# A fused retention and mixture-of-experts layer: routing at the end of VectorE's rounds, expert biases loaded ahead of rows, and one normalisation ahead of the last expert slot's activations

## The reference, cut to what matters

```python
xn = layernorm(x)
q, k, v = xn @ W_q.T, xn @ W_k.T, xn @ W_v.T              # 16 heads of 16
attn = einsum('bihd,bjhd->bhij', q, k) * decay / sqrt(16) # decay: gamma_h ** (i - j), causal
y = einsum('bhij,bjhd->bihd', attn, v)
yn = (y - y.mean((1, 3))) / sqrt(y.var((1, 3)) + eps)     # over time and head width
a = (yn * gn_weight + gn_bias) @ W_o.T
probs = softmax(xn @ gate_w.T + gate_b); top 2 of 8
f = sum over the two experts of prob * (relu(xn @ w1[e] + b1[e]) @ w2[e] + b2[e])
out = x + a + f
```

## Time and profile before

| what | us |
|---|---|
| median of 3 runs | 731.72 (730.7 to 731.83) |
| the profiled execution's own time | 733.6 |
| its span | 731.2 |
| PE busy | 694.6 (95%) |
| DVE busy | 579.1 (79%) |
| ACT busy | 486.0 (66%) |
| mean granted TensorE clock | 0.994 of full speed |

### The profile page before, as it was taken

One profiled execution on the slowest core, in us unless ns is written; L12 is line 12 of the kernel. 1 busy time (PEld: TensorE's weight loads), 2 busy tenths in 40 slices (PEclk: granted clock), 3 DMA queues, 4 the chain that ended last, 5 costly groups with the idle time before them and its releaser, 6 DMA issues.

```text
span 731.2 us, 19479 instructions
## 1 busy us (share of the span) xinstructions
PE 694.6 (95%) x6564; PEld 652.8 (89%) x6564; DVE 579.1 (79%) x1090; ACT 486.0 (66%) x883; POOL 287.4 (39%) x229
## 2 busy tenths in 40 slices
PE   3899999999999999999999999999999999999976
PEld 2677777887888999999999999999999999999975
DVE  6778889887887896887787878787878787888655
ACT  3645433443445887878787787878787878788690
POOL 3300006688650143543535353535344444434200
PEclk9999999999999999999999999999999999999999
DMA  9960113533750978787878788878887888878249
GB/s 303 373 234 31 58 52 116 167 117 124 238 180 7 372 187 252 204 268 193 264 195 262 199 256 223 232 230 230 233 230 234 223 245 214 261 186 264 34 144 324
DMA packets 67632, 149.17 MB, mean 204 GB/s; under 512 B 12560, under 2 KB 46096, under 8 KB 57488
## 3 DMA queue, kind: packets, MB, share of 16 engines
q1 hardware_dynamic: 53872, 130.53, 52.4%
q0 software_dynamic: 13728, 18.23, 15.2%
HBM read 111.22 MB, written 36.46 MB: 202 GB/s over the span
## 4 chain that ended last, share of the span: by engine, by line
PE 67%; DMA 11%; issue 9%; DVE 6%; POOL 3%; ACT 3%; SPq 1%; DVEq 0%; POOLq 0%; ACTq 0%
PE ps L816 26%; PE ps L731 25%; DMA xs_rows<-xn_rows,rows 6%; PE ps L778 3%; DMA sum_rows<-arena_f,pair_slot 2%; PE ps L993 2%; PE ps L800 2%; PE ps L864 2%; PE ps L843 2%; PE ps L854 1%; POOL sum_rows L490 1%; DMA xn_rows<-x 1%; PE ps L787 1%; PE ps L824 1%; POOL xs_rows L470 1%
## 5 line engine op out<-in xcount | busy, mean ns | idle before, releaser
L816 PE MATMUL ps<-arena_r 128*128 128x256 f32 (+1 forms) x1872 | 229.7, 282 | 0.3 <-DVE arena_r L1234 0.3
L731 PE MATMUL ps<-arena_r 128*128 128x256 f32 x1776 | 224.2, 286 | 3.0 <-DVE arena_r L1331 3.0
L816 PEld LDWEIGHTS ps<-arena_r 128*128 128x128 f32 x1872 | 225.9, 192 | 0.7 <-issue 0.7
L731 PEld LDWEIGHTS ps<-arena_r 128*128 128x128 f32 x1776 | 216.9, 193 | 4.0 <-DVE arena_r L1331 2.4
L488 POOL TENSOR_TENSOR fence_out<-eps_col 128x1 f32<-128x1 f32 x39 | 77.9, 1998 | 273.7 <-DVE arena_f L1301 273.7
L542 ACT ACTIVATE arena_r<-arena_f 128x2048 fp32r<-128x2048 f32 x77 | 143.7, 1920 | 0.2 <-DMA arena_f<-w 0.2
L490 POOL DMA_INDIRECT sum_rows<-arena_f,pair_slot x74 | 118.9, 1606 | 16.6 <-issue 15.5
L655 ACT ACTIVATE arena_f<-ps,arena_f 128x256 f32<-128x256 f32 (+1 forms) x156 | 63.8, 461 | 88.7 <-PE ps L816 69.5
L1322 DVE TENSOR_TENSOR arena_r<-arena_f,arena_r 128x2048 fp32r<-128x2048 f32 x39 | 89.3, 2291 | 32.2 <-ACT arena_r L542 32.1
L1216 DVE TENSOR_TENSOR arena_f<-ps,cst 128x512 f32<-128x512 f32 x128 | 84.6, 683 | 6.3 <-PE ps L843 5.8
L1331 DVE TENSOR_TENSOR arena_r<-arena_f,arena_r 128x512 fp32r<-128x512 f32 (+1 forms) x78 | 53.3, 686 | 44.3 <-ACT arena_r L664 44.2
(11 more groups left out here) (156 smaller groups left out, 837.4 us busy)
## 6 DMA issues: line engine op xcount, KB each, us to landing
arena_f<-w SPq DMA_DIRECT2D x78, 1024.0 KB, 5.7
xs_rows<-spare_rows SPq DMA_DIRECT2D x35, 260.0 KB, 3.9
arena_f<-xs_rows SPq DMA_DIRECT2D x35, 260.0 KB, 3.1
arena_f<-b SPq DMA_DIRECT2D x39, 128.0 KB, 3.1
xn_rows<-x SPq DMA_DIRECT2D x8, 512.0 KB, 9.0
sum_rows<-x SPq DMA_DIRECT2D x8, 512.0 KB, 3.8
arena_f<-sum_rows SPq DMA_DIRECT2D x8, 512.0 KB, 7.5
out<-arena_f SPq DMA_DIRECT2D x16, 256.0 KB, 6.4
```

The costliest lines, as they stand in the source:

```text
L731: last = pe.matmul(out_ap, lhs(a), rhs(b), start=start and n == 0, stop=stop and n == 2, **kw)
L816: last = pe.matmul(ps[:, H_BANK[hp], o * rows:(o + 1) * rows], w1_r[par][:, a, at:at + P], xs_r[:, b, k * rows:(k + 1) * rows], start=(m = ...
```

## The change

It has three parts.

1. VectorE's routing pieces stand at the end of a round, behind the fourth masked score, where they stood behind `new_state`. They begin in round 0 rather than 1, so each piece but the last runs one round earlier; `gate_values` gets round 4 of its own, and both `rows_of_pairs` run in round 10. `counts_after` lies at another place of the same buffer, since its old place is overwritten by the output of tile 8.
2. SyncE issues the biases of slot sl+1 ahead of the rows of slot sl+2.
3. ScalarE normalises half batch 0 and makes its high part ahead of the `hidden` steps of the last slot (38), and VectorE runs `ys_gated` of that slot ahead of `low_half(1)`.

```diff
@@ -200,7 +200,7 @@
 
         w_raw = [ff(KC * cols) for cols in (2 * D, D, D)]
         x_grp_t = ff(2, KC, GRP * P)
-        counts_after = x_grp_t[:, 0, 0, 0:NT * E].rearrange("p (t e) -> p t e", t=NT)
+        counts_after = x_grp_t[:, 1, 1, NT * E:2 * NT * E].rearrange("p (t e) -> p t e", t=NT)
         ones_te = x_grp_t[:, 0, 1, 0:NT * E]
         logit_t = sb("logit_t", [P, 2, P])
         stats = sb("stats", [P, 2, GRP, 6])
@@ -417,9 +417,10 @@
             def slot_step(sl, par):
                 if within(sl + 2, NS):
                     weights_load(sl + 2, par)
-                    rows_load(sl + 2, par)
                 if within(sl + 1, NS):
                     bias_load(sl + 1, 1 - par)
+                if within(sl + 2, NS):
+                    rows_load(sl + 2, par)
 
             run_steps(sp, 0, NS, 2, NBIG - 3, slot_step)
 
@@ -663,10 +664,32 @@
                 rows = P * row_tiles(sl)
                 nc.scalar.activation(h_r[:, 0, hp * 2 * rows:(hp + 1) * 2 * rows], h_f[hp][:, 0:2 * rows], ACT.Copy).then_inc(s["h_h"], 1)
 
+            scale = gn_ab[:, 0].rearrange("p b h c -> p (b h) c")
+            shift = gn_ab[:, 1].rearrange("p b h c -> p (b h) c")
+
+            def norm_scale(hb):
+                for c in range(KC):
+                    nc.scalar.activation(y_t[:, hb * 4:hb * 4 + 4, c], y_t[:, hb * 4:hb * 4 + 4, c], ACT.Identity,
+                                         scale=scale[:, hb:hb + 1, c], bias=shift[:, hb:hb + 1, c]).then_inc(s["yn_f"], 1)
+
+            def norm_high(hb):
+                act.wait_ge(s["yn_f"], hb * 2 + 2)
+
+                wait(act, s["o_psum"], hb - 3)
+                nc.scalar.activation(yn_r[hb % 4][:, 0].rearrange("p c (t i) -> p t c i", t=4), y_t[:, hb * 4:hb * 4 + 4],
+                                     ACT.Copy).then_inc(s["yn_h"], 1)
+
             def slot_step(sl, par):
                 if within(sl + 1, NS):
                     w_high(0, sl + 1, 1 - par)
+                if isinstance(sl, int) and sl == NS - 1:
+                    act.wait_ge(s["gn_ab"], 2)
+                    act.wait_ge(s["y_home"], 16)
+                    norm_scale(0)
                 act.wait_ge(s[f"bias_in{par}"], (sl - par) * 16 + 32)
+                if isinstance(sl, int) and sl == NS - 1:
+                    act.wait_ge(s["ys_psum"], NS - 1)
+                    norm_high(0)
                 hidden(sl, par, 0)
                 for hp in range(1, FC // 2):
                     hidden(sl, par, hp)
@@ -698,27 +721,9 @@
                 slot_step(sl, sl % 2)
 
 
-            act.wait_ge(s["gn_ab"], 2)
-
-            act.wait_ge(s["ys_psum"], NS - 1)
-            scale = gn_ab[:, 0].rearrange("p b h c -> p (b h) c")
-            shift = gn_ab[:, 1].rearrange("p b h c -> p (b h) c")
-
-            act.wait_ge(s["y_home"], 16)
-
-            def norm_half(hb):
-
-                for c in range(KC):
-                    nc.scalar.activation(y_t[:, hb * 4:hb * 4 + 4, c], y_t[:, hb * 4:hb * 4 + 4, c], ACT.Identity,
-                                         scale=scale[:, hb:hb + 1, c], bias=shift[:, hb:hb + 1, c]).then_inc(s["yn_f"], 1)
-                act.wait_ge(s["yn_f"], hb * 2 + 2)
-
-                wait(act, s["o_psum"], hb - 3)
-                nc.scalar.activation(yn_r[hb % 4][:, 0].rearrange("p c (t i) -> p t c i", t=4), y_t[:, hb * 4:hb * 4 + 4],
-                                     ACT.Copy).then_inc(s["yn_h"], 1)
-
-            for hb in range(2 * B):
-                norm_half(hb)
+            for hb in range(1, 2 * B):
+                norm_scale(hb)
+                norm_high(hb)
 
 
         @block.tensor
@@ -1158,14 +1163,16 @@
                 V.tensor_copy(expert_of[:], slot_expert[:]).then_inc(s["route_done"], 1)
 
             def routing(i):
-                if i == 1:
+                if i == 0:
                     shifted_logits()
+                elif i == 1:
+                    first_expert()
                 elif i == 2:
-                    first_expert()
+                    next_peaks()
                 elif i == 3:
-                    next_peaks()
+                    second_expert()
                 elif i == 4:
-                    second_expert()
+                    gate_values()
                 elif i == 5:
                     tokens_upto()
                     tokens_of_experts()
@@ -1179,9 +1186,8 @@
                     rows_of_halves()
                 elif i == 10:
                     rows_of_pairs(0)
-                    gate_values()
+                    rows_of_pairs(1)
                 elif i == 11:
-                    rows_of_pairs(1)
                     experts_of_slots()
 
 
@@ -1248,8 +1254,6 @@
                     tokens_low(i + 1, 1 - par)
                 if within(i - 1, NT - 1):
                     new_state(i - 1)
-                if route:
-                    routing(i)
                 if stats > 1:
                     output_stats(i - LATE, early=True)
                 if isinstance(i, int) and i == NT - 1:
@@ -1268,6 +1272,8 @@
                     queries(i + 1, 1 - par)
                 if within(i, NT):
                     masked_scores(i, 3)
+                if route:
+                    routing(i)
 
 
             for g in range(-1, NG):
@@ -1413,8 +1419,8 @@
                     V.tensor_tensor(pair, pair, ps[:, hb % 3 * 2 + q, :], ALU.add).then_inc(s["out_sb"], 1)
 
             low_half(0)
+            ys_gated(NS - 1, (NS - 1) % 2)
             low_half(1)
-            ys_gated(NS - 1, (NS - 1) % 2)
             low_half(2)
             low_half(3)
             for hb in range(2 * B):
```

## The result

The changed kernel takes 794.62 us (median of 6 runs, 787.86 to 806.7), the kernel before beside it 731.74. The ratio is 1.0812, with a 95% interval of 1.0761 to 1.0863: **8% slower**. Forecast were 722.9 us.

A forecast was written before the change was run, and what follows sets the result against it. TensorE, busy 95% of the span, bounds the kernel, so time is gained where it idles or something else carries the end. 4.6 + 0 + 4.24 = 8.84 us off 731.72 gives 722.9 us; 8 in 10 range 720.5 to 726.0.

The forecast's parts named there:

- Part 1: Attention: routing pieces hide behind VectorE's existing waits, so GpSimd's scatters start at 106.4 instead of 111.02, 4.6 us gained.
- The two long pieces: Attention: the `rows_of_pairs` pair in round 10 and `experts_of_slots` in round 11 delay their chunks, charged 0.7 us each.
- Part 3: Last slot and output: `ys_gated(38)` starts at about 695.05 instead of 699.29, 4.24 us gained, as the DMA chain ends last.
- At the same distances: End of kernel: scatter, loads and first addition follow the earlier `ys_gated(38)` as before; TensorE's fourth half batch at 705.4.
- The wait before that half batch: Output: TensorE waits for the first additions before its fourth half batch, from 703.6 to 705.4, 1.8 us.
- Part 2: Slots: early biases end ScalarE's bias waits, priced at zero; bounds from a gain of 1.33 us to a loss of 2.
- The slack of 0.87 us: Slot 34: `hidden_low(0)` is done at 639.25 and `layer2` starts at 640.12, room a delayed scatter must exceed to cost time.
- The rival that happened: Every slot: earlier w1 load and biases delay scatters beyond slot 34's slack; 0.3 us beyond costs 9.9, time 732.8, chance 0.03.
- Against: ScalarE waits for DMA only 7 times: Slots: argument against the slower rival, that ScalarE waits for DMA only 7 times in 39 slots, all for biases.
- The biases: Slots: ScalarE's bias waits, 15.9 us in 7 places, go at no gain; slot 36's TensorE wait of 1.33 us stays.
- The clock: TensorE: a wait sometimes costs about 1.3 us more at half rate; rival before the fourth half batch, 724.2 us, chance 0.13.

The follow-up runs named there:

- three reads: The changed kernel with three unused reads of the expert number behind each rows load, holding back the next w1 load: 723.75 us, ratio 0.9865.
- parts 1 and 3 alone: The changed kernel with the old order of SyncE's loads, rows ahead of biases: 725.31 us, ratio 0.9908 to the kernel before.

## Why the prediction was wrong

- **Part 1** was right: `inside(10)` at 104.48 (forecast 104.19), GpSimd at 106.49 (106.4), tile 20 still waiting, 2.14 us. The two long pieces delay the projection by 0.55 and 0.92 us, where 0.7 each was charged. Alone it measures 6.2 us in the medians, 4.3 in the spans, for a term of 4.6.
- **Part 3** was right in its first step, 7.61 - 3.37 = 4.24 us. "At the same distances" was not. From `ys_gated(38)` to TensorE's fourth half batch it took 709.64 - 699.29 = 10.35 us; now 783.19 - 771.80 = 11.39. GpSimd's fence is the cause that the trace names (below): 1.09 us in place of 0.19, which is 0.90 of these 1.04. The wait before that half batch is 3.15 us, where 1.8 was forecast.
- **Part 2** is the step that failed, with its price of zero: "Where a scatter's landing holds `ys_gated` (slots 3 to 5) this can add some tenths", with a loss of at most 2 us. The w1 load did come earlier, by some 2 us rather than 1.1 in such a slot (0.9 to 1.35 behind the second scatter, where slots 2 to 4 before have 2.96 to 3.27). From second scatter to `ys_gated` it took 8.36 us (median) instead of some 6, in slot after slot, and part 2 cost some 66 us (1.0812 - 0.9908 of 732). The step took the three waits at the start for a local matter. They were the same closed circle, in a kernel just able to leave it: 6.03, 7.07, 5.95 and 4.71 us from second scatter to `ys_gated`, around the edge of 6.06.
- **The slack of 0.87 us** The earlier trace rows was read in slot 34, far out in the free state, and taken to be what an early w1 load must use up. Free slots do have room: with w1 at 3.1 us the time is unharmed. The changed kernel never reaches that state. What had to be compared was the landing with 6.06 us in slots 2 to 5.
- **The rival that happened** is the slower one, with a chance of 0.03 and a price of 9.9 us. Its mechanism was right in that the early w1 load delays the scatter in nearly every slot; its price was about one seventh of the 66 us, since it reckoned 0.3 us beyond the slack for each slot by itself, where a slot of the closed circle is 2.3 us longer (470.4 - 393.8 over 33). "Against: ScalarE waits for DMA only 7 times" looked at the wrong engine; VectorE's row of waits for the scatter, 7.2 us in 3 slots, was there to be read and is in no group of rows.
- **The biases** did what was said: ScalarE's waits for them fell from 15.9 us to 1.5, and that is worth nothing that could be measured (three reads 0.9865, parts 1 and 3 alone 0.9908, intervals overlapping). TensorE's 1.3 us wait of slot 36 stays in these kernels.
- **The clock** cost more than the one stretch reckoned with. After the 3.20 us wait at 395.80 the 48 matmuls took 7.33 us in place of 6.0, at a granted clock of 0.77 from 396 to 402, so at 1.2 GHz for part of the stretch and at 2.4 for the rest. Busy times, clock, DMA share and GB/s of that stretch:

```profile
396.00:402.00 6.00, 6.00 (x40) 6.00 (x41) 4.87 (x9) 2.16 (x2) 3.23 (x2) 0.77 0.67 152
```

  Many such waits make the 17.3 us of slower `layer2`.

## What to carry to other kernels

Where a transfer's landing releases an engine, and that engine releases both the next such transfer and a large load, look for a circle: write down the fixed distances, and compare the landing with the pace of the bounding engine less that distance. Near that edge half a microsecond of issue time decided some 65 us here, and slack read from a slot in the free state says nothing of the closed one. A few waits at the start that die out are the sign that the edge is near; and of a list of DMA issues, moving one item moves all that stand behind it.
